# The written order of the attention block and of the layers' first eight steps is drawn anew

## The chip, the cores and the metric

The kernel runs on one core of one Trainium2 chip. The metric is the device time of one execution in microseconds (us), the median of several runs. The engines of the core are TensorE (PE; its weight loads are listed apart as PEld), VectorE (DVE), ScalarE (ACT), GpSimd (POOL) and SyncE (SP), which issues all the DMAs of this kernel. An engine works through its own instructions in their written order; between engines only semaphores order the work.

## What is computed

x has 8 sequences of 1024 rows of 256 numbers. A causal attention block with one head of 64 comes first, then a layer norm; then two layers of local attention (8 heads of 64, windows of 128 rows, each window looks at itself and the one before) with a gated feed-forward part; then a last layer norm. Cut from the reference:

```python
# the attention block
q = x @ wq + bq; k = x @ wk + bk; v = x @ wv + bv
w = softmax(q @ k.T / sqrt(64) + causal_mask)
x = layernorm(x + (w @ v) @ wo + bo)
# two layers, l = 0 and 1
qkv = shift_token(x) @ wqkv[l]
q = rotary(l2norm(q) * q_scale[l]); k = rotary(l2norm(k) * k_scale[l])
x = x + local_attention(q, k, v) @ wo[l]          # window 128 and the one before
h = layernorm(shift_token(x)) * ln_g[l] + ln_b[l]
a, g = split(h @ w1[l] + b1[l])
x = x + (a * gelu(g)) @ w2[l] + b2[l]
# the end
x = layernorm(x1 + x)                              # x1: the input of the layers
```

## The kernel before

All of x is cut into tiles of 128 rows. The attention block works by sequence b (0 to 7) and window j or half n; the layers work by tile T(g), g = 0 to 127: 64 tiles for each of the two layers, and Q(g) is the pair of tiles g and g + 1, which the wide feed-forward products take together.

Each engine has a set of small functions (calls), one for one step of work on one tile. `attention` (from line 188) defines those of the attention block, `layers` (from line 607) those of the layers. On TensorE, the attention has turn_x (transposes of x, L481), project_qk (L491), project_v (L501), scores (L514 and L515), turn_probs (L522), values (L533) and output (L543). scores(b, 4n) waits for the copies of k: ScalarE writes k's high half (k_high), VectorE its low half (k_low), and SyncE copies both to the other 64 partitions (k_high_again at L255, k_low_again at L260). output is followed on VectorE by y_sum (L451), and the next output waits for it, since there is one bank for it. Two banks, turn[0] and turn[1], are shared by turn_x, project_qk, project_v and turn_probs, and each use of one waits until the last one has been read (the waits on `done` in the list).

In the layers TensorE has turn_x (L2486), project_k, project_q, project_v, turn_q, turn_k, scores, turn_probs (L2540), values (L2551), output, turn_h (L2568), widen (in six parts) and narrow. Products of the layers are made of three matmuls each, of high and low halves (`three_pass`, L173 to L175). VectorE takes the rope (rope_cos, rope_sin), norms, the low halves (x_low, q_low, k_low, o_low, h_low, gated_low), least_of for the scores, middle, the statistics and x_new; ScalarE the high halves, the squares, exponentials and gelu; GpSimd inverse_norms, k_sum, k_scaled, normalise and residual.

While the attention runs, the weights of both layers are brought in: SyncE loads them raw (load_raw, L265), ScalarE makes the high half (raw_high), GpSimd the low half (raw_low, L345), SyncE stores both (store_split, L270 and L271), and loads the first layer's part back (load_qkv; first_weights after the attention's last store). The tables of the rope are made on GpSimd (rope_table, L352) and those of the second layer stored (store_tables, L321). Some tiles of the layers lie where tiles of the attention lay. Waits (guards) in the calls of tile 0 keep the order: k_high waits for the stored tables, v_out, probs_out and least_of for all stored splits, o_high, middle and zero_tail for all rows of x1 stored. The second layer's own weight tiles (`next_q_h` and the five like it, loaded by load_next at L756 and following) lie where tiles of the attention lay too.

The order of the work is written out by hand, as a list of calls, for the attention block and the beginning of the layers: `first_on_sync` (L3432), `first_on_gpsimd` (L3691), `first_on_scalar` (L3958), `first_on_vector` (L4535) and `first_on_tensor` (L5468). The last has 727 calls with 647 waits between them. Then `all_steps` runs the function `step` of each engine, from step 8 on SyncE and GpSimd, 9 on ScalarE and VectorE and 11 on TensorE, up to 59, two tiles a step, and `last_steps` is written out again.

## Time and profile before

| | us |
|---|---|
| median of 3 runs | 2685.9 |
| lowest and highest | 2682.23 and 2689.82 |
| the profiled execution | 2684.28 |
| its span, first to last instruction | 2682.5 |
| mean granted TensorE clock | 0.993 |
| TensorE busy, share of the span | 98% |
| VectorE, ScalarE, GpSimd busy | 85%, 72%, 62% |

Busy times are those of the profiled execution. Matmuls are pipelined and their ends are modelled, so that the record of one matmul is longer than the time from its start to the start of the next. Times in the rows below count from the start of the span.

### The profile page before, as it was taken

To read this page: it belongs to the slowest core of one execution; us is meant where nothing else is said; L and a number is where in the kernel's file an instruction comes from. 1 tells how busy PE (TensorE), PEld (TensorE's weight loads), DVE (VectorE), ACT (ScalarE), POOL (GpSimd) and SP (SyncE) were. 2 spreads that over 40 slices of the span, in tenths; PEclk is the share of its full clock that TensorE was granted. 3 is DMA by queue.
4 is the path that set the end of the run, shared out by engine and by line. 5 is a ranking of instruction groups with operands and counts; after the bars stand their busy time and mean duration, and the time that the engine had idled before them with its cause. 6 is when DMAs were issued, how large, how long until landed. Compare 5 with 4: busy or idle time off the path is not lost.

```text
span 2682.5 us, 65519 instructions
## 1 busy us (share of the span) xinstructions
PE 2626.4 (98%) x22240; PEld 2309.2 (86%) x22240; DVE 2276.5 (85%) x6866; ACT 1934.8 (72%) x4826; POOL 1658.1 (62%) x1753
## 2 busy tenths in 40 slices
PE   8999999999999999999999999999999999999998
PEld 5677688899998899998999898989988999988887
DVE  5778988888888888888888889898989989998786
ACT  5655588777777777777777777777777777778775
POOL 6523755566566556666665676666766667766563
PEclk9999999999999999999999999999999999999999
DMA  9931300000001100000001211011101111111110
GB/s 314 334 105 59 107 21 24 29 24 29 27 27 55 44 25 29 25 29 24 28 25 60 93 31 36 30 37 33 37 30 34 33 33 37 31 36 34 30 32 23
DMA packets 144510, 140.37 MB, mean 52 GB/s; under 512 B 16024, under 2 KB 126128, under 8 KB 143408
## 3 DMA queue, kind: packets, MB, share of 16 engines
q1 hardware_dynamic: 144176, 136.18, 16.0%
q8 instruction: 177, 2.90, 0.4%
q14 instruction: 157, 1.29, 0.2%
HBM read 80.02 MB, written 51.92 MB: 49 GB/s over the span
## 4 chain that ended last, share of the span: by engine, by line
PE 61%; DVE 2%; ACT 1%; issue 1%; DMA 1%; SPq 0%; POOL 0%; DVEq 0%; ACTq 0%; POOLq 0%
PE p_pair L173 13%; PE p_pair L174 10%; PE p_pair L175 10%; PE p_values L2551 6%; PE p_turn L2540 5%; PE p_mixed L173 4%; PE p_mixed L175 4%; PE p_mixed L174 4%; PE p_turn L2522 2%; PE p_turn L2516 1%; PE p_mixed L2486 1%; PE p_mixed L2568 1%; PE p_mixed L2594 0%; PE p_mixed L2593 0%; ACT prob L1224 0%
## 5 line engine op out<-in xcount | busy, mean ns | idle before, releaser
L960 POOL TENSOR_TENSOR prob<-prob,rinv 128x512 f32<-128x512 f32 (+1 forms) x512 | 506.5, 1001 | 393.0 <-DVE rinv L1771 392.7
L1224 ACT ACTIVATE prob<-prob,least 128x256 f32<-128x256 f32 (+1 forms) x1024 | 496.2, 487 | 63.2 <-DVE least L1763 61.7
L938 POOL TENSOR_TENSOR inv_norm<-norm_clipped,minus_half 128x8 f32<-128x8 f32 x256 | 423.0, 1659 | 79.2 <-DVE norm_clipped L1727 71.8
L1763 DVE CUSTOM_DVE_ANT_0 prob<-p_pair,mask,inv_norm 128x256 f32<-128x256 f32 (+1 forms) x1024 | 440.2, 460 | 35.0 <-PE p_pair L175 33.0
L173 PE MATMUL p_pair<-hT_h,w_h 128*128 128x256 f32 (+1 forms) x1408 | 410.1, 291 | 6.9 <-ACT v L1218 2.5
L174 PE MATMUL p_pair<-hT_l,w_h 128*128 128x256 f32 (+1 forms) x1408 | 391.1, 278 | 0.0
L175 PE MATMUL p_pair<-hT_h,w_l 128*128 128x256 f32 (+1 forms) x1408 | 391.0, 278 | 0.0
L1236 ACT ACTIVATE pT<-p_turn 128x512 f32<-128x512 f32 (+1 forms) x512 | 283.7, 569 | 76.3 <-PE p_turn L2540 63.9
L173 PEld LDWEIGHTS p_pair<-hT_h,w_h 128*128 128x128 f32 (+1 forms) x1408 | 262.6, 186 | 22.7 <-issue 10.8
L1835 DVE SCALAR_TENSOR_TENSOR gated<-p_pair,columns,gelu 128x256 f32<-128x256 f32 (+1 forms) x384 | 184.0, 481 | 108.5 <-ACT gelu L1263 106.4
L2540 PE MATMUL p_turn<-ident,prob 128*128 128x128 f32 x1920 | 266.5, 273 | 0.8 <-POOL prob L960 0.5
L174 PEld LDWEIGHTS p_pair<-hT_l,w_h 128*128 128x128 f32 (+1 forms) x1408 | 262.9, 187 | 0.0
L175 PEld LDWEIGHTS p_pair<-hT_h,w_l 128*128 128x128 f32 (+1 forms) x1408 | 262.2, 186 | 0.0
L2551 PE MATMUL p_values<-pT,v 128*64 128x128 f32 x3840 | 248.7, 277 | 1.0 <-ACT pT L1236 0.9
L2540 PEld LDWEIGHTS p_turn<-ident,prob 128*128 128x128 f32 x1920 | 220.6, 140 | 26.2 <-issue 10.4
L2551 PEld LDWEIGHTS p_values<-pT,v 128*64 128x64 f32 x3840 | 206.1, 137 | 28.4 <-issue 9.6
L1843 DVE TENSOR_TENSOR gT_l<-gated,gT_h 128x256 fp32r<-128x256 f32 (+1 forms) x384 | 187.6, 490 | 40.1 <-ACT gT_h L1280 38.9
L1263 ACT ACTIVATE gelu<-p_pair,columns 128x256 f32<-128x256 f32 x320 | 150.7, 473 | 92.1 <-PE p_pair L175 91.3
L1711 DVE TENSOR_TENSOR rope_sin<-p_pair,rope_tab 128x256 f32<-128x256 f32 x512 | 199.2, 412 | 0.0
L1224 ACT ACTIVATION_READ_ACCUMULATOR prob<-prob,least 128x1 f32 x1024 | 195.0, 190 | 0.0
L1720 DVE TENSOR_REDUCE norms_sq<-squares 128x8 f32<-128x512 f32 x256 | 173.9, 679 | 24.1 <-ACT squares L1193 23.6
L173 PE MATMUL p_mixed<-w_h,gT_h 128*128 128x256 f32 x640 | 183.4, 287 | 6.1 <-DVE gT_l L1843 3.4
(147 smaller groups left out, 7970.3 us busy)
## 6 DMA issues: line engine op xcount, KB each, us to landing
x_tile<-x_rows SPq DMA_DIRECT2D x192, 128.0 KB, 2.1
a_wraw<-in_w_all SPq DMA_DIRECT2D x32, 264.0 KB, 5.3
w_high<-a_wraw_h SPq DMA_DIRECT2D x32, 264.0 KB, 3.9
w_low<-a_wraw_l SPq DMA_DIRECT2D x32, 264.0 KB, 4.7
a_x<-in_x SPq DMA_DIRECT2D x32, 256.0 KB, 4.2
x_rows<-a_x SPq DMA_DIRECT2D x64, 128.0 KB, 1.8
x_tile<-x_rows SPq DMA_DIRECT2D x128, 64.0 KB, 2.0
mid_rows<-x_mid SPq DMA_DIRECT2D x128, 64.0 KB, 1.7
```

The costliest lines, as they stand in the source:

```text
L173: pe.matmul(out, lh, rh, start=start, stop=False)
L174: pe.matmul(out, lh, rl, start=False, stop=False)
L175: return pe.matmul(out, ll, rh, start=False, stop=stop)
L938: pool.tensor_tensor(r[:, t.slot(2), heads], rt[:, heads], half[:, heads], ALU.pow).then_inc(pool_r[n], 1)
L960: pool.tensor_tensor(p, p, rinv[:, 2 * m:2 * m + 2].unsqueeze(2).to_broadcast([P, 2, cols.stop - cols.start]), ALU.mult).then_inc(pool_p, 1)
L1224: act.activation(prob[:, h, cols], prob[:, h, cols], ACT.Exp, bias=least[:, h:h + 1], scale=-1.0, accum_out=rsum[:, h:h + 1]).then_inc(act ...
L1236: act.activation(pT[:, 2 * m:2 * m + 2, blocks, :], src[:, :, blocks, :], ACT.Copy).then_inc(act_pT, 1)
L1711: ins = dve.tensor_tensor(dst[:, :, s], src[:, :, 1 - s], table[:, 2 * n + 1, s].unsqueeze(1).to_broadcast([P, H, D // 2]), ALU.mult)
L1763: dve.tensor_tensor_reduce(prob[:, h, cols], p_score[h % 2][:, c0 + cols.start:c0 + cols.stop], mask[:, a.slot(2), cols], r[:, a.slot(2), ...
L1843: dve.tensor_tensor(gT_l[0:rows, n], gt[0:rows, n % 3], gT_h[0:rows, n].bitcast(F32), ALU.subtract).then_inc(dve_gT, 1)
L2540: ins = pe.transpose(p_turn[m % 2][:, (2 * hh + b) * P:(2 * hh + b + 1) * P], prob[:, 2 * m + hh, b * P:(b + 1) * P], ident[:])
L2551: ins = pe.matmul(p_val[half_ * D:(half_ + 1) * D, m * P:(m + 1) * P], v[:, slot, h * D:(h + 1) * D], pT[:, h, b], start=b == blocks[0], s ...
```

## The change

Only the five written lists are changed, and the first step of the loop on SyncE. No call is added or taken away: each list has the same calls as before in another order (SyncE's has eight more, which are those of its step 8, and its loop begins at 9). The waits in the list of TensorE go with the calls: each call waits for what its banks and inputs need in the new order. From turn_x(T(13)) on TensorE's list is as it was.

```diff
@@ in post_norm_block @@
-            all_steps(t.step, 8, 60)
+            all_steps(t.step, 9, 60)
@@ first_on_sync @@
     a.load_ident()
+    a.load_bvo()
     a.load_x(0, 0)
-    a.load_wqk()
     a.load_x(0, 1)
     a.load_x(0, 2)
     a.load_x(0, 3)
     a.load_wo()
-    a.load_cmask()
-    a.load_bvo()
+    a.load_wqk()
+    a.load_x(1, 0)
     a.load_wv()
-    a.load_tables()
     a.load_raw(0, 0)
     a.load_raw(0, 1)
+    a.load_tables()
+    a.load_x(1, 1)
     a.load_raw(0, 2)
     a.load_raw(0, 3)
+    a.store_split(0, 0)
+    a.load_x(1, 2)
+    a.load_cmask()
     a.k_high_again(0, 0)
-    a.load_x(1, 0)
-    a.k_high_again(0, 1)
-    a.k_low_again(0, 0)
-    a.load_x(1, 1)
-    a.load_x(1, 2)
-    a.load_x(1, 3)
-    a.k_low_again(0, 1)
-    a.load_x(2, 0)
-    a.store_split(0, 0)
     a.load_raw(1, 0)
-    a.load_shared()
-    a.load_x(2, 1)
     a.load_raw(1, 1)
     a.store_split(0, 1)
+    a.k_low_again(0, 0)
+    a.k_low_again(0, 1)
+    a.load_x(1, 3)
+    a.load_x(2, 0)
+    a.load_x(2, 1)
+    a.k_high_again(0, 1)
     a.load_raw(1, 2)
+    a.load_shared()
     a.load_raw(1, 3)
+    a.load_raw(2, 0)
+    a.load_raw(2, 1)
     a.store_split(0, 2)
-    a.load_raw(2, 0)
     a.store_split(0, 3)
     a.store_split(1, 0)
+    a.store_split(1, 1)
+    a.k_low_again(1, 0)
+    a.store_tables()
     a.k_high_again(1, 0)
```

On TensorE, the head of the new list, where project_v now comes ahead of project_qk:

```python
a.turn_x(0, 0, turn[0])          # as before up to turn_x(0, 3)
...
a.project_v(0, 0, turn[0])
pe.wait_ge(done.xT_done, 4)
a.project_v(0, 1, turn[1])
pe.wait_ge(done.v_done, 1)
a.project_qk(0, 0, turn[0])
pe.wait_ge(done.v_done, 2)
a.project_qk(0, 1, turn[1])
pe.wait_ge(done.kl_done, 1)
a.turn_x(1, 0, turn[0])
pe.wait_ge(done.kl_done, 2)
a.turn_x(1, 1, turn[1])
```

From project_qk(1, 1) to scores(1, 4) in the new list (waits left out; in the old one project_v(1, 1), output(1, 0), project_v(2, 0), project_qk(2, 0), output(1, 1) and turn_probs(1, 2) stood between them):

```python
a.project_qk(1, 1, turn[0])
a.values(0, 6)
a.turn_probs(0, 7, 0, turn[1])
a.output(0, 4)
a.turn_probs(0, 7, 1, turn[1])
a.turn_probs(1, 0, 0, turn[0])
a.output(0, 5)
a.values(0, 7)
a.turn_probs(1, 1, 0, turn[1])
a.turn_probs(1, 2, 0, turn[0])
a.output(0, 6)
a.values(1, 0)
a.scores(1, 4)
```

At the attention's end, the projections of tile 0 and turn_q(T(0)) now stand ahead of scores(7, 5), where they stood behind turn_probs(7, 5), and scores(T(0), 0) stands ahead of output(7, 6), where it stood behind output(7, 7). On GpSimd all rope tables are made ahead of raw_low(1, 2); the last one stood behind raw_low(2, 0). On SyncE the loads of x for tiles 0 to 3 stand behind load_x(3, 1), where they stood behind store_x1(2, 3) and later.

## Rows read from the trace of the kernel before

**Rows 1.** Busy by stretch of 67 us: PE, PEld, DVE, ACT, POOL, PEclk, DMA, GB/s.

```profile
0.00:67.00 67.00, 54.69 (x318) 39.63 (x319) 36.25 (x104) 38.22 (x76) 44.69 (x57) 0.95 0.95 313
67.00:134.00 67.00, 63.20 (x419) 46.30 (x418) 51.22 (x156) 45.57 (x97) 37.05 (x39) 0.95 0.97 334
134.00:201.00 67.00, 62.87 (x448) 47.08 (x446) 49.74 (x159) 36.25 (x78) 20.00 (x27) 0.95 0.34 105
...
268.00:335.00 67.00, 60.56 (x453) 46.50 (x452) 60.74 (x188) 39.22 (x116) 49.62 (x50) 0.95 0.30 107
...
536.00:604.00 68.00, 68.00 (x582) 61.24 (x582) 58.51 (x179) 49.95 (x131) 40.90 (x42) 1.00 0.09 25
```

**Rows 2.** TensorE's waits up to 700 us: line <- releaser, us, times, longest.

```profile
PE p_turn L481 <- DMA a_x<-in_x: 8.1, 3, 3.9
PE p_mixed L543 <- DVE a_y L451: 5.1, 7, 1.7
...
PE p_pair L514 <- DMA a_k_low_twice<-a_k_low_twice: 2.4, 3, 1.8
```

**Rows 3.** Timeline from 9 us: start, duration, engine, line, operation [idle before it].

```profile
14.61 0.59 SPq L247 DMA_DIRECT2D a_x<-in_x  x1
...
15.78 0.59 SPq L260 DMA_DIRECT2D a_k_low_twice<-a_k_low_twice  x1
...
22.03 0.90 PE L481 MATMUL p_turn<-ident,a_x 128*128 128x128 f32 x4 [2.72 <-DMA a_x<-in_x]
...
23.31 0.44 PE L514 MATMUL p_pair<-a_k_high_twice,a_q_high_low 128*128 128x128 f32 x1 [0.38 <-DMA a_k_low_twice<-a_k_low_twice]
```

**Rows 4.** Busy by microsecond behind that wait; the third number from the end is PEclk.

```profile
23.00:24.00 1.00, 0.69 (x3) 0.72 (x4) 0.00 (x0) 0.56 (x1) 1.00 (x2) 0.50 1.08 355
...
30.00:31.00 1.00, 1.00 (x12) 1.00 (x11) 0.39 (x4) 0.71 (x1) 1.00 (x1) 1.00 1.06 406
```

**Rows 5.** Timeline of TensorE: project_qk(1, 0), and two matmuls of a layer's projection.

```profile
33.48 1.88 PE L491 MATMUL p_turn<-a_xT,a_wqk 128*128 128x512 f32 x4
...
1003.09 0.40 PE L173 MATMUL p_pair<-wqkv_h,xT_h 128*128 128x512 f32 x1
1003.33 0.39 PE L174 MATMUL p_pair<-wqkv_l,xT_h 128*128 128x512 f32 x1
```

**Rows 6.** Timeline of TensorE: turn_x of tiles 0, 13, 14 and 16.

```profile
244.61 0.42 PE L2486 MATMUL p_mixed<-ident,x_tile 128*128 128x128 f32 x2
...
481.83 0.38 PE L2486 MATMUL p_mixed<-ident,x_tile 128*128 128x128 f32 x2
506.57 0.38 PE L2486 MATMUL p_mixed<-ident,x_tile 128*128 128x128 f32 x2
...
543.73 0.38 PE L2486 MATMUL p_mixed<-ident,x_tile 128*128 128x128 f32 x2
```

**Rows 7.** VectorE up to 300 us, by line: busy us, mean ns, idle before.

```profile
L451 DVE SCALAR_TENSOR_TENSOR a_y<-p_mixed,a_rinv,a_x_plus_bo 128x256 f32<-128x256 f32 x64 | 30.7, 480 | 11.5 <-PE p_mixed L543 5.7 <-issue 5.4
```

**Rows 8.** Busy by stretch at the attention's end, columns as in group 1.

```profile
270.00:280.00 10.00, 6.45 (x47) 4.60 (x46) 9.78 (x27) 1.68 (x3) 5.84 (x6) 0.91 0.11 39
280.00:290.00 10.00, 9.46 (x68) 6.97 (x66) 9.89 (x38) 6.66 (x24) 6.28 (x9) 0.92 0.29 92
```

**Rows 9.** Timeline from 80 us: project_qk(2, 1), table store, k copy, scores(2, 4).

```profile
81.16 1.98 PE L491 MATMUL p_turn<-a_xT,a_wqk 128*128 128x512 f32 x4
81.59 0.61 SPq L321 DMA_DIRECT2D rope_tables<-a_tab_layer  x1
...
86.98 0.48 SPq L260 DMA_DIRECT2D a_k_low_twice<-a_k_low_twice  x1
...
92.56 0.47 PE L514 MATMUL p_pair<-a_k_high_twice,a_q_high_low 128*128 128x512 f32 x1 [1.76 <-DMA a_k_low_twice<-a_k_low_twice]
```

**Rows 10.** The copies of k's low half in the whole run, from issue to landing.

```profile
DMA to landing us min/median/max: 2.2/3.3/7.4
```

**Rows 11.** DMA issues of the first 150 us: KB each, median us to landing.

```profile
a_k_low_twice<-a_k_low_twice SPq DMA_DIRECT2D x10, 128.0 KB, 4.5
```

More of the change, by code:

```diff
@@ L5491, in first_on_tensor @@
     a.turn_x(1, 2, turn[0])
+    pe.wait_ge(done.xT_done, 6)
+    a.project_v(1, 0, turn[1])
+    a.scores(0, 0)
+    a.scores(0, 1)
+    pe.wait_ge(done.xT_done, 7)
+    a.project_qk(1, 0, turn[0])
+    pe.wait_ge(done.v_done, 3)
+    a.turn_x(1, 3, turn[1])
     a.scores(0, 2)
@@ L5554, in first_on_tensor @@
+    a.scores(1, 5)
+    a.values(1, 1)
     a.output(0, 7)
[L5555 to L5569 removed]
@@ L5588, in first_on_tensor @@
-    pe.wait_ge(done.pT_done, 17)
+    a.turn_x(2, 1, turn[1])
+    a.scores(1, 7)
+    a.values(1, 2)
+    pe.wait_ge(done.xT_done, 9)
+    a.turn_probs(1, 4, 0, turn[0])
+    a.output(1, 0)
+    pe.wait_ge(done.xT_done, 10)
+    a.project_qk(2, 0, turn[1])
+    a.values(1, 3)
+    pe.wait_ge(done.pT_done, 17)
+    a.project_v(2, 0, turn[0])
+    a.output(1, 1)
+    pe.wait_ge(done.kl_done, 5)
+    a.turn_probs(1, 4, 1, turn[1])
+    a.output(1, 2)
+    pe.wait_ge(done.v_done, 5)
     a.turn_probs(1, 5, 0, turn[0])
-    a.output(1, 3)
@@ L5744, in first_on_tensor @@
+    a.project_v(4, 1, turn[1])
+    a.output(3, 6)
+    a.values(4, 0)
+    pe.wait_ge(done.pT_done, 50)
     a.turn_x(5, 0, turn[0])
-    pe.wait_ge(done.pT_done, 48)
+    a.scores(4, 6)
+    pe.wait_ge(done.v_done, 10)
     a.turn_x(5, 1, turn[1])
-    a.values(3, 7)
-    a.output(3, 6)
+    a.output(3, 7)
+    a.values(4, 1)
+    a.scores(4, 7)
     pe.wait_ge(done.xT_done, 21)
-    a.turn_x(5, 2, turn[0])
+    a.turn_probs(4, 2, 0, turn[0])
     pe.wait_ge(done.xT_done, 22)
-    a.project_qk(5, 0, turn[1])
@@ new lines, in first_on_tensor @@
+    pe.wait_ge(done.pT_done, 58)
+    a.project_qk(5, 0, turn[1])
+    pe.wait_ge(done.pT_done, 59)
+    a.project_qk(5, 1, turn[0])
+    a.output(4, 5)
+    a.values(4, 6)
+    pe.wait_ge(done.kl_done, 11)
+    a.turn_probs(4, 7, 1, turn[1])
+    a.output(4, 6)
+    pe.wait_ge(done.kl_done, 12)
+    a.turn_x(6, 0, turn[0])
+    a.values(4, 7)
+    pe.wait_ge(done.pT_done, 60)
+    a.turn_x(6, 1, turn[1])
+    a.scores(5, 0)
+    pe.wait_ge(done.xT_done, 25)
+    a.turn_x(6, 2, turn[0])
+    a.scores(5, 1)
@@ L5953, in first_on_tensor @@
-    pe.wait_ge(done.v_done, 16)
-    a.turn_probs(7, 3, 0, turn[1])
-    a.values(7, 2)
+    t.project_k(T(0), 0)
+    a.values(7, 0)
+    pe.wait_ge(done.v_done, 15)
+    a.turn_probs(7, 1, 0, turn[0])
+    pe.wait_ge(done.v_done, 16)
+    a.turn_probs(7, 2, 0, turn[1])
+    a.scores(7, 4)
+    t.project_k(T(0), 1)
+    a.output(7, 0)
+    a.values(7, 1)
+    pe.wait_ge(done.pT_done, 86)
+    a.turn_probs(7, 3, 0, turn[0])
+    pe.wait_ge(done.s_low, 60)
+    t.after((signal.dve_xT, T(0), 1, 1))
@@ L6048, in first_on_tensor @@
     t.turn_probs(T(0), 3)
+    t.after((signal.dve_xT, T(2), 1, 1))
+    t.turn_x(T(3))
+    pe.wait_ge(done.zT_done, 64)
+    t.after((signal.act_pT, T(0), 4, 1))
+    t.values(T(0), 0)
+    t.after((signal.act_pT, T(0), 4, 2))
+    t.values(T(0), 1)
     t.after((signal.dve_kr, T(2), 1, 1))
@@ L6261, in first_on_tensor @@
+    t.scores(T(6), 1)
+    t.after((signal.dve_hv, Q(2), 1, 1))
+    t.narrow(T(0))
     t.after((signal.act_pT, T(5), 4, 1))
```

3010 lines of the change are left out of this document (1474 added, 1536 removed).

## The prediction

> **What bounds the kernel now.** I read four views, in this order. First the busy times of stretches of 67 us [rows 1]: TensorE is busy all the time from 536 us on, and the places where it is not (12.3 us idle in the first stretch, 3.8 in the second, 4.1 in the third, 6.4 in the fifth) all lie in the part whose order is rewritten. Second, who ended TensorE's idle time there [rows 2]: loads of x, the attention's y, the copy of k's low half. Third, the clock: after the 2.72 us of idle time that end at 22.03 us [rows 3] the granted clock reads 0.50, the lower of its two levels (1.2 GHz for 2.4), and 1.00 again by 30 us [rows 4]. Four of the first five stretches of 67 us have a mean of 0.95 [rows 1]: 0.05 x 67 x 4 = 13.4 us of work not done.
>
> Fourth, a count, because busy time is too coarse for a change that moves calls and removes none. I give each TensorE call the time between its first matmul and the next call's in dense rows: 0.235 us for a 512-column three-pass matmul, so 1.45 for a whole projection; 1.75 for project_qk and 1.9 for the attention's project_v, read like them [rows 5]; found in the same way: scores of window j 0.10 + 0.117(j + 1), values 0.10 + 0.06(j + 1), a transpose 0.115, output 0.5 in the attention and 1.46 in the layers, widen 1.42, narrow 2.05. The 727 written calls make 507.5 us in either order. Over two tiles of the steady part the count gives 37.4 us, and the trace 37.16 (506.57 to 543.73 [rows 6]), so it can be trusted to 1%. Time of the trace minus work counted is the **slip** of TensorE. It is 54.0 us at tile 0's turn_x (244.61 - 190.6), 83.3 at tile 13's (481.83 - 398.5) and 83.1 at tile 16's (543.73 - 460.6) [rows 6]: all of it arises before tile 13, and from tile 13's turn_x on both orders are the same, call by call. Of the 83, some 34 are idle time and 13 the clock; about 36 are waits too short for a row of their own, switches between kinds of matmul, and errors of my call times in the attention. So the change can win at most some 45 to 50 us and will surely leave most of them.
>
> The Trainium skill says in "Perfetto Trace Analysis", section "Identifying the Most-Contended Engine", that occupancy of the matmul row is no measure of headroom, while that of VectorE is. The trace agrees: in the fifth stretch TensorE is 90% busy [rows 1], and the slip still grows by some 12 us. By busy time alone the sum below would have a ceiling of some 34 us, by the slip one of 83.
>
> **VectorE in the written order.** I count VectorE the same way, with the mean times of its groups (0.48 for a y_sum [rows 7], 0.46 + 0.08 for a least of the layers, and so on), and take for each wait of TensorE the VectorE work written up to the result that it waits for, minus the TensorE work written before the call. This **lead** may rise and fall without harm as long as VectorE has idle time; where it rises and VectorE is full, TensorE slips by the rise. In the old order it is 1.6 us or less for the first 140 us of work, 9.3 at the turn_x of tile 1, 24.3 at project_v of tile 2 and 33.5 at its highest, project_v of tile 9. VectorE is indeed 98% and 99% busy from 270 to 290 us [rows 8], and the slip rises there from 57 to 69 us.
>
> **The change, part by part** (sum against the profiled execution: 2684.28 us with a span of 2682.5; the median of the three runs, 2685.9, is 1.6 above it).
>
> *The first 30 us.* project_v now goes ahead of project_qk. The biases that it needs (160 KB) are issued ahead of x(0,0), which delays that by one issue, about 0.45 us; wqk moves behind four loads of x and two of wo and still lands before it is needed; x(1,0) is issued before all raw weights and not behind them (before: issued at 14.61, waited for until 22.03 [rows 3]). Going through the calls by hand, with 0.68 us for each half of q or k on ScalarE and 0.75 on VectorE (their groups' means), turn_x(1,0) starts at about 18.6 with 9.2 us of work behind it (slip 9.4; before 12.8), and scores(0,0) at 24.0 if the k copies have landed. They are issued at about 19.4 behind raw loads and splits; the first low copy took 7.5 us before (15.78 to 23.3 [rows 3]), so they land between 24 and 27. The slip there is 11.5 to 14.5; the old order has 15.9 at 13.9 us of work. Gain 1.4 to 4.4 us; I take **-3.0**, the middle.
>
> *The copies of k.* scores(b, 4n) needs both halves of k copied, and the work written between project_qk(b, n) and it is the cover. The chain can be timed at (2,1): from the end of the product (81.16 + 1.98) to the copy's arrival (92.5) 9.4 us, 5.6 of them the low half's own flight, and scores(2,4) waited 1.76 us [rows 9] with a stretch of low clock behind it (3.3 us of work). This came right behind the 1 MB store of the rope tables (81.59 [rows 9]), which now goes out some 50 us earlier. The flight is 2.2 us at least and 7.4 at most, its median 3.3 over the run [rows 10] and 4.5 in the first 150 us [rows 11], where the DMA engines are full [rows 1]. (2,1) keeps its cover (6.7 us, now 6.8): with 4.5 its chain is 8.3 and the wait shrinks to some 0.6, mostly without the clock; -5.0 if all goes, 0 if all stays, I take -4. (1,1) had 6.95 us of cover and now 4.6, stretched by the usual slip to 5.4: with 4.5 a wait of 2.9, and the clock's 3.3 may follow; between 0 (flight 2.2) and 4.0 + 3.3 (chain as at (2,1)). I take 2.9 and half the clock's, +4.5. (3,0) falls from 9.4 to 5.8, (5,0) from 11.2 to 5.3 and (6,1) from 9.1 to 4.5, but from 134 us on the DMA engines are a third busy or less, and the old (4,0) had 5.2 without a row of idle time: +1.5 together, between 0 and 6. The part: **+2.0**, between -5 and +13.
>
> The Trainium skill's "DMA: Bandwidth & Descriptors", section "Queues, rings and completion order", has the descriptors of one queue on one engine start in order. The trace agrees (15.78 to 23.3 us for a copy behind a load [rows 3]). It speaks against this part, as SyncE now issues k_high_again(0,1) behind three loads of x.
>
> *The rest of the attention.* Outputs that follow each other too closely for the y between them (under 0.9 us of work) fall from nine to seven; turn_x to the projections gets shorter in places. No row prices this: **0**, between -3 and +3, from the 5.1 us that outputs waited for y in all [rows 2].
>
> *From the attention's end to tile 13.* The lead rises from 10.2 (output(7,2)) to 32.5 (turn_q of tile 6), by 22.3 us, before from 9.3 to 33.5, by 24.2. At project_v of tile 3 it is 25.9, in the old order 23.7. VectorE's work is the same and it is full here, so most of this slip stays: **-2.0**, between -6 (the small waits of 0.8 to 1.1 us after 350 us go too) and +3 (tile 2's project_k has 0.7 us of work behind its turn_x, before 2.0, and ScalarE and VectorE need 0.8 in between by their groups' means).
>
> *Hidden edits.* The rope tables on GpSimd (16 x 0.73 us) move ahead of raw_low of the second batch; SyncE waits for the last of them in store_tables, with k_high_again(1,0) queued behind it, but scores(1,0) now has 10.5 us of cover for 6.3. The loads of x for tiles 0 to 3 and the last wqkv loads move within the time before 150 us, and their first reader is at 240 us. The first layer weights, loaded from 290 us on, still wait for the attention's last store, with nothing reordered around it. The eight calls of step 8 on SyncE are written out and not looped. All at 0; if a cover failed, a load's flight of 2 to 4 us.
>
> Sum: -3.0 + 2.0 + 0 - 2.0 = -3.0, so 2681.3 us by the profiled execution and 2682.9 beside the median. **I predict 2682 us**, between the two, its own range 2676 to 2690.
>
> **The rivals.** (A) *The low clock goes as well.* If neither the load of x nor the k copies stop TensorE for over 1.5 us at a stretch, three stretches of low clock vanish (3.35 us of work each) with 2.72 + 1.76 us of idle time before two of them and 1.2 before the third: 15.7 in all, of which the attention's end gives back some 3 because VectorE is full: 2684.3 - 12.7 = 2671.6, and beside the median 2673 us. For it: the gaps before 22 and 92.6 us have one cause each, and both are moved. Against: shorter cover for k. (B) *The k copies become the bound, slower than before.* If they fly 5 us or more behind the raw loads, (1,1) and (3,0) each wait 2.5 to 3 us and drop the clock (3.3), 12 us for the two, scores(2,4) waits as before, and the copy for scores(0,0) lands at 27 us, which leaves 1.4 of the head's gain: +12 - 1.4 - 2 (the layers) = +8.6, 2694.5 us beside the median. It decides from a flight of 4.5 us on; the median of the whole run is below that [rows 10], that of the first 150 us upon it [rows 11]. (C) *VectorE keeps all.* What the attention gains is given back by 300 us, since VectorE has 39 us of work there for 26 of TensorE's: 2686 us, no change.
>
> **How the numbers follow.** My forecast 0.37, C 0.20, A 0.27, B 0.16. A measurement of this kernel can tell about 0.3% (8.1 us) from no change: faster means below 2677.8, slower above 2694.0. Nearly all of A is faster, with a little of the forecast's edge, 0.29; most of B is slower with little else, 0.14; the rest is 0.57. For 8 times in 10 the range takes in A's middle and B's near half: 2670 to 2695.
>
> **What the profile would show.** Right: no idle time of over 1 us on a load of x near 22 us; a wait of TensorE on the k copy at scores(1,4) of 2 to 4 us, and at most a small one at scores(2,4); VectorE over 95% busy around 270 to 290 us; tile 13's turn_x at a slip of 79 to 82 us, which is 478 to 480 us in the trace; from there on the same 37.16 us for two tiles. Wrong: a new wait on a k copy in each batch, or a store or load on SyncE that stands in front of them; a low clock that stays away altogether; a change of the steady part, on which everything here is set to zero.

## The result, and the profile after

The changed kernel takes 2697.3 us in the median of six executions (2689.5 to 2701.1), the old one 2685.4 beside it (2682.2 to 2689.8). The ratio is 1.0038 with a 95% interval of 1.0026 to 1.0049: **slower** by 7 to 13 us. The forecast was 2682, between 2670 and 2695, with 0.14 for slower.

The profiled execution of the changed kernel took 2689.5 us and is the fastest of its six, so a good part of the loss is not in it. Its page:

```profile
span 2687.7 us, 65516 instructions
...
PE 2618.9 (97%) x22240; PEld 2307.1 (86%) x22240; DVE 2276.1 (85%) x6866; ACT 1929.1 (72%) x4820; POOL 1658.1 (62%) x1753
```

The transposes (turn_x) of tiles 0, 13, 14 and 16 in the timeline of TensorE answer to [rows 6] (start, duration, engine, line):

```profile
240.54 0.38 PE L2486 MATMUL p_mixed<-ident,x_tile 128*128 128x128 f32 x2
...
485.17 0.38 PE L2486 MATMUL p_mixed<-ident,x_tile 128*128 128x128 f32 x2
...
509.89 0.38 PE L2486 MATMUL p_mixed<-ident,x_tile 128*128 128x128 f32 x2
...
547.03 0.38 PE L2486 MATMUL p_mixed<-ident,x_tile 128*128 128x128 f32 x2
```

By the count of the prediction tile 0 stands behind 188.2 us of work in the new order, tiles 13, 14 and 16 behind 398.5, 423.2 and 460.6 as before. The slip is 240.54 - 188.2 = 52.4 us at tile 0 (old 54.0), 86.6 at tile 13 (old 83.3) and 86.4 at tile 16. So here the attention is 1.6 us better, **the layers' first 13 tiles are 5.0 us worse** (34.3 us of slip against 29.3), and the steady part still takes 37.14 us for two tiles. All along the loop from there to tile 126 the two traces keep 2.6 to 3.8 us apart. The last 2 us come at the very end, where the last products of the new trace run at a lower granted clock (0.81 from 2670 to 2680 us, old 1.00) on the same instructions.

TensorE's waits between 300 and 485 us, old kernel first, then the changed one (line <- releaser: us in all, times, longest):

```profile
PE p_pair L173 <- ACT v L1218: 1.9, 2, 1.1
PE p_pair L173 <- DVE rope_sin L1711: 1.4, 2, 0.8
PE p_pair L173 <- DVE gated L1835: 1.1, 1, 1.1
PE p_mixed L173 <- DVE x_new L1855: 0.5, 1, 0.5
```

```profile
PE p_pair L173 <- DVE gated L1835: 3.2, 3, 1.7
PE p_pair L173 <- ACT v L1218: 2.2, 1, 2.2
PE p_pair L173 <- DVE rope_sin L1711: 2.0, 4, 0.8
PE p_pair L173 <- DVE kT_l L1746: 1.2, 1, 1.2
PE p_pair L173 <- DVE least L1763: 1.0, 2, 0.7
PE p_pair L173 <- DVE xT_l L1691: 1.0, 1, 1.0
PE p_turn L2540 <- POOL prob L960: 0.9, 1, 0.9
```

With the small ones that are left out, 5.7 us of waits became 14.0. The slip rose by 5.0 only, so some of them stand in the place of waits too short for a row. None is long; they are spread over all three engines that read TensorE's banks. But they do not weigh the same. At the transposes of tile 11 the slip is some 80 us in the new trace (430.59 us, behind 351 of work) and some 82 in the old one (437.95, behind 356): the new order is still ahead. From there to tile 13 it grows by some 7 us, in the old trace by 1. In the 20 us behind tile 11's transposes ScalarE is full, and VectorE and TensorE are not (new trace, columns as in [rows 1]):

```profile
430.00:440.00 10.00, 8.26 (x76) 6.98 (x72) 8.93 (x30) 9.88 (x19) 6.86 (x8) 1.00 0.01 2
440.00:450.00 10.00, 7.28 (x54) 5.87 (x54) 5.44 (x17) 9.90 (x21) 2.62 (x3) 1.00 0.01 2
```

In the same 20 us of the old trace TensorE is full, and VectorE nearly so:

```profile
430.00:440.00 10.00, 10.00 (x86) 8.97 (x86) 9.79 (x24) 6.00 (x15) 8.49 (x7) 1.00 0.16 48
440.00:450.00 10.00, 10.00 (x82) 8.44 (x79) 9.68 (x30) 9.19 (x22) 3.34 (x5) 1.00 0.13 35
```

The old order has such a stretch too, from 410 to 430 us (ScalarE 97% and 96% busy, TensorE 89% and 91%). The two largest waits of the new trace stand 4 us apart:

```profile
434.96 0.47 ACT L1263 ACTIVATE gelu<-p_pair,columns 128x256 f32<-128x256 f32 x1
...
435.94 1.28 ACT L1224 ACT_TABLE_LOAD   x1
...
438.16 1.28 ACT L1263 ACT_TABLE_LOAD   x1
...
439.46 0.47 ACT L1263 ACTIVATE gelu<-p_pair,columns 128x256 f32<-128x256 f32 x1
...
439.96 0.48 DVE L1835 SCALAR_TENSOR_TENSOR gated<-p_pair,columns,gelu 128x256 f32<-128x256 f32 x1
...
440.50 0.50 PE L173 MATMUL p_pair<-wqkv_h,xT_h 128*128 128x512 f32 x1 [1.73 <-DVE gated L1835]
...
443.57 0.71 ACT L1280 ACTIVATE gT_h<-gated 128x256 fp32r<-128x256 f32 x2
...
444.18 0.58 ACT L1218 ACTIVATE v<-p_pair 128x512 f32<-128x512 f32 x1
...
444.81 0.37 PE L173 MATMUL p_pair<-hT_h,w_h 128*106 128x256 f32 x1 [2.21 <-ACT v L1218]
```

Read from the bottom: the sixth widen product of tiles 4 and 5 needs the bank of tile 10's v, which ScalarE copies out at 444.18, behind two exponentials, a k_high and two gated_high, though the last matmul of the product was done by 442.2 (441.77 + 0.39). And v's own product could start only at 440.50, since its bank held a widen product whose gated was late, whose gelu had waited for two table loads on **ScalarE**. In the old list project_v(T(10)) stood in front of the third widen product, here it stands between the fifth and the sixth.

### The profile page after: what moved, and what is told of

Its sections match the earlier page's. It is cut to its first block, busy times and chain, and to the rows that moved or that the text cites. A ratio compares the mean times of both kernels' runs of the same rounds, so it can differ in the third digit from the quotient of the medians.

```text
span 2687.7 us, 65516 instructions
## 1 busy us (share of the span) xinstructions
PE 2618.9 (97%) x22240; PEld 2307.1 (86%) x22240; DVE 2276.1 (85%) x6866; ACT 1929.1 (72%) x4820; POOL 1658.1 (62%) x1753
## 4 chain that ended last, share of the span: by engine, by line
PE 61%; DVE 2%; ACT 2%; issue 1%; DMA 1%; SPq 0%; POOL 0%; DVEq 0%; ACTq 0%; POOLq 0%
PE p_pair L173 13%; PE p_pair L174 10%; PE p_pair L175 10%; PE p_values L2551 6%; PE p_turn L2540 5%; PE p_mixed L173 4%; PE p_mixed L175 4%; PE p_mixed L174 4%; PE p_turn L2522 2%; PE p_turn L2516 1%; PE p_mixed L2486 1%; PE p_mixed L2568 1%; PE p_mixed L2594 0%; PE p_mixed L2593 0%; ACT prob L1224 0%
## 5 line engine op out<-in xcount | busy, mean ns | idle before, releaser
L1224 ACT ACTIVATE prob<-prob,least 128x256 f32<-128x256 f32 (+1 forms) x1024 | 495.9, 487 | 60.1 <-DVE least L1763 58.6
L173 PEld LDWEIGHTS p_pair<-hT_h,w_h 128*128 128x128 f32 (+1 forms) x1408 | 262.7, 187 | 21.7 <-issue 10.3
```

The source lines that it names most:

```text
L173: pe.matmul(out, lh, rh, start=start, stop=False)
L1224: act.activation(prob[:, h, cols], prob[:, h, cols], ACT.Exp, bias=least[:, h:h + 1], scale=-1.0, accum_out=rsum[:, h:h + 1]).then_inc(act ...
```

## The experiments

For each trace I worked out the slip as in the prediction, from the turn_x of tiles 0, 6 and 13 and the order in the kernel's list. This table holds the study's traces (A: attention, L: layers from the output product of tile 0 on; "new" with an edit is marked):

| trace | A, L | slip at tile 0 | 0 to 6 | 6 to 13 |
|---|---|---|---|---|
| before | old, old | 54.0 | 17.4 | 11.9 |
| before_look | old, old | 52.0 | 19.5 | 12.2 |
| short_before | old, old | 53.9 | 17.4 | 11.8 |
| after | new, new | 52.4 | 18.0 | 16.3 |
| after_again | new, new | 55.2 | 18.0 | 16.3 |
| after_look2 | new, new | 61.3 | 18.0 | 16.3 |
| after_look3 | new, new | 55.6 | 18.0 | 16.3 |
| short_after | new, new | 58.2 | 18.0 | 16.3 |
| att_after_lay_before | new, old | 58.9 | 17.4 | 12.2 |
| old_layers_look | new, old | 58.4 | 17.1 | 12.2 |
| old_layers_look2 | new, old | 59.0 | 15.8 | 12.2 |
| att_before_lay_after | old, new | 54.2 | 23.8 | 16.3 |
| restore_from_tile5 | new, new to tile 5 | 54.0 | 25.6 | 13.8 |
| v10_early | new, new edited | 60.0 | 19.9 | 18.4 |
| gelu_grouped | new, new edited | 55.9 | 19.1 | 21.0 |
| head_alone | old with new head, old | 57.2 | 17.3 | 11.9 |
| old_head | new with old head, new | 60.2 | 18.0 | 16.3 |
| bvo_later | new edited, new | 57.2 | 18.0 | 16.3 |
| warm_start | new edited, new | 58.6 | 18.0 | 16.3 |
| old_layers_warm | new edited, old | 59.2 | 15.8 | 12.2 |

### Where the loss is: the lists cut and joined

At some points the calls written so far are the same set in both orders, on each engine. There a list of the one order can go on as the other.

```diff
 # att_after_lay_before (att_before_lay_after: the other way round)
 def first_on_tensor: new order up to t.output(T(0)), t.turn_k(T(2)), t.turn_probs(T(1), 0)
-    (new) t.values(T(1), 0), t.turn_probs(T(1), 1), t.turn_probs(T(1), 2), ...
+    (old) t.values(T(1), 0), t.turn_probs(T(1), 1), t.scores(T(2), 0), ...
 # restore_from_tile5: the same behind t.project_v(T(5))
```

after_again, the changed kernel as it is:

> The changed kernel once more, nothing edited. Its median stood at 2697.3 us (six executions, 2689.5 to 2701.1) and its one profiled execution at 2689.5, so some 8 us of the loss are in no trace yet. Theory L (layers): the loss is fixed work order in tiles 5 to 12 of the layers; then the spread is chance, the median comes again at 2695 to 2699, and a second trace shows tile 13's transposes at 484 to 487 us. Theory K (copies of k): the loss is in the attention and changes with how long the copies of k take to land; then a slower profiled execution has the transposes of tile 0 later than 240.5 us by about what it is slower.

Measured: 2697.7 us, ratio 1.0037 (1.0025 to 1.0049); the profiled execution 2692.8. The loss repeats. The trace is 2.8 us later than the first at tile 0, and from there equal to it within 0.1 us: both theories had a part right, the layers cost a fixed amount and the attention a varying one.

> The changed kernel up to the output product of the layers' tile 0 (about 300 us), from there the old order on all five engines. Theory L: the waits of 1.7 and 2.2 us for gated and v near 440 us go, tile 13's transposes come 3 to 5 us earlier than in the changed kernel (480 to 482 us), and the time is 2692 to 2694 us. Theory K: what is lost is lost before 300 us, and the time stays at 2696 to 2698.

Measured: 2686.7 us, ratio 1.0002 (0.9993 to 1.0010). **The whole loss is gone with the old order of the layers**, and more of it than theory L asked for.

```profile
247.05 0.38 PE L2486 MATMUL p_mixed<-ident,x_tile 128*128 128x128 f32 x2
...
486.93 0.38 PE L2486 MATMUL p_mixed<-ident,x_tile 128*128 128x128 f32 x2
```

Tiles 0 and 13 in its trace: 239.88 us apart, in the changed kernel 244.63. In the table this is 29.6 us of slip against 34.3. But this trace took 2692.3 us, the slowest of its eleven.

> The mirror image: the old order up to the output product of the layers' tile 0, from there the new one. Theory L: 2689 to 2692 us, with the waits near 440 us in the trace. Theory K: 2685 to 2688 us, since the old attention has its copies of k in time.

Measured: 2696.6 us, ratio 1.0038 (1.0026 to 1.0050). The new layers bring the loss along with the old attention: for L, against K. The time is 5 us above what L said, and the trace shows why this kernel is no clean measure: it loses 23.8 us between tiles 0 and 6, where the pure orders lose 17.4 (19.5 in before_look) and 18.0. Some 1.5 us of the excess arise ahead of the join, where the clock is low for longer (from 278 to 288 us, as in before_look), the rest behind it. From tile 6 on it has the 16.3 of the new order.

> The changed kernel with the old order restored only from about the value product of the layers' tile 5 on (370 us), so that only the stretch with the waits near 440 us is as before. Theory L: as the kernel restored from tile 0 on, 2692 to 2694 us, and tile 13's transposes at 480 to 482 us. Theory K: 2696 to 2698 us.

Measured: 2698.1 us, ratio 1.0046 (1.0034 to 1.0058). By itself this would say K. The trace says otherwise: 25.6 us between tiles 0 and 6 (18.0 without a join), with the excess at the join (a wait of 2.7 us for x_mid with a stretch of low clock behind it), and then 13.8 in place of 16.3. The experiment is spoilt by its join and settles nothing on size.

### Why executions of one kernel differ

> The changed kernel once more, for a trace of one of its slower executions. Its two traces so far (2689.5 and 2692.8 us) took 19.3 to 21.1 us less of TensorE work away between the transposes of tiles 2 and 6 than time went by less than the mixed kernel did, and lie below the median of 2697.5. Theory W (waits of the layers' tiles 2 to 6): a slower execution loses 4 to 7 us more between the transposes of tiles 2 and 6 (time beyond counted work 8.3 in both traces, then 13 to 15, as in the kernel with the old attention and the new layers), by waits and a lower clock together. Theory K: it loses them before tile 0's transposes (52.4 and 55.2 us beyond counted work, then 58 to 60).

> The same kernel and the same two theories as the run before it: W puts what is above 2692 us between the transposes of tiles 2 and 6, K ahead of tile 0's.

(The first text has a muddled sentence; what counts in it is 8.3 us between tiles 2 and 6 for W and 58 to 60 at tile 0 for K.) Measured: 2698.3 and 2692.6 us. All five traces of the new order have 18.0 and 16.3 us, to 0.1; the slow one has 61.3 us at tile 0. **W is wrong, K right** as to where the variation arises, ahead of tile 0. But it isn't the copies of k: up to 245 us TensorE waits 3.6 us for them in the slow trace and 3.9 in the changed kernel's first one, while its waits for pT ahead of turn_probs go from 1.9 to 4.7 us. Part of the variation arises in the first 25 us. TensorE's timeline there, the changed kernel's first trace and then after_look2 (v is L501, q and k L491):

```profile
6.25 3.74 PE L481 MATMUL p_turn<-ident,a_x 128*128 128x128 f32 x16 [6.25 <-DMA a_x<-in_x]
...
9.99 3.92 PE L501 MATMUL p_turn<-a_wv,a_xT 128*128 128x64 f32 x32
13.75 3.65 PE L491 MATMUL p_turn<-a_xT,a_wqk 128*128 128x512 f32 x8
18.81 0.66 PE L481 MATMUL p_turn<-ident,a_x 128*128 128x128 f32 x4 [1.41 <-DVE a_k_low_twice L416]
```

```profile
10.60 7.06 PE L501 MATMUL p_turn<-a_wv,a_xT 128*128 128x64 f32 x32 [0.34 <-DMA a_wv<-in_wv]
17.45 6.24 PE L491 MATMUL p_turn<-a_xT,a_wqk 128*128 128x512 f32 x8
24.31 0.66 PE L481 MATMUL p_turn<-ident,a_x 128*128 128x128 f32 x4 [0.62 <-DVE a_k_low_twice L416]
```

The same 32 matmuls take 3.92 or 7.06 us, 0.12 or 0.22 each. Of the 15 traces that begin with the new head, seven have 3.8 to 4.1 us, seven 7.06, and one (warm_start) 4.59. The slow heads reach their next transposes at 22.8 to 24.3 us, 4.0 to 5.5 later. The old head has no such levels: its five traces have 4.3 to 5.2 us for q and k and 2.00 for the first 16 matmuls of v. What the pace is, the traces tell (last section): it is the granted clock, whose record opens with full speed at 9.5 to 11.0 us in the seven heads with v in 3.8 to 4.1 us, at 18.7 to 22.6 in the seven with 7.06 and at 11.3 to 12.4 in the five old ones.

Two more edits and the mirror image of the head were to show whether this makes the times.

```diff
 # head_alone: old kernel, new order of the first calls (TensorE 8, SyncE 31, GpSimd 15, ScalarE 12, VectorE 7)
 # old_head: the changed kernel with the old order of the same calls
 # bvo_later, first_on_sync
-    a.load_bvo()
     a.load_x(0, 0)
     a.load_x(0, 1)
     a.load_x(0, 2)
     a.load_x(0, 3)
+    a.load_bvo()
 # warm_start, turn_x(0, 0), behind the wait for the identity (old_layers_warm: new attention
 # and old layers, with 6 of them and bvo_later's edit)
+                for m in range(14):
+                    pe.transpose(turn[1][:, m % 4 * P:(m % 4 + 1) * P], ident[:], ident[:])
```

> The old kernel with the new order of the head alone: on all engines up to the first sequence's q, k and v products (first 8 calls on TensorE, 31 on SyncE, 15 on GpSimd, 12 on ScalarE, 7 on VectorE); the first two transposes after it wait for the low half of k as well. My forecast's step: the head gives 1.4 to 4.4 us, so 2681.5 to 2684.5. The rival: bvo ahead of x(0,0) holds the first transposes 2.3 us later and k comes after v, so it gives nothing or costs up to 3 us, 2686 to 2689.

Measured: 2687.7 us beside 2686.0, ratio 1.0007 (0.9998 to 1.0016); 57.2 us of slip at tile 0, v in 7.06 us. The head gives nothing; whether it costs is within the interval (-0.5 to +4.3 us). The rival's side.

> The changed kernel with one call of SyncE moved: bvo is loaded behind the four pieces of x of the first sequence, no longer ahead of them. In the traces of the changed kernel the first transposes start at 6.1 to 6.7 us (old kernel: 3.95), and the 32 matmuls of the first v products take either 3.8 to 4.1 us or 7.06 us. Theory P (pace of the head): whether TensorE works at full pace at 10 us or only at 20 us makes the two levels of the changed kernel's times (2689 to 2693 and 2697 to 2701); with work from 4 us on it is at full pace by 12 us, the slow level goes, and the median falls to 2688 to 2692. Rival: only the 2.3 us of later start count, and the median falls to 2694 to 2696 with both levels left.

Measured: 2692.3 beside 2683.2 on this chip, ratio 1.0034 (1.0022 to 1.0045). The first transposes start at 4.07 us, as said, but v takes 7.06 us all the same. An earlier start doesn't bring the full pace. The ratio is hardly under that of the changed kernel.

> The changed kernel with 14 transposes of the identity added on TensorE ahead of the first transposes of x, while it waits for x anyway (from 2.6 us, when the identity is there, to about 6 us). They compute nothing that is used. Theory P: TensorE has been at work from 2.6 us on, the first v products take 3.8 to 4.1 us in the trace, the slow level goes, and the median is 2689 to 2693. Rival: the two levels have another cause, and the median stays at 2696 to 2699.

Measured: 2694.8, ratio 1.0040 (1.0023 to 1.0057), executions from 2687.0 to 2702.3. TensorE was at work from 2.80 us, v took 4.59 us, and then q and k 6.22, at the low pace. The added work did bring full pace early, from 6.8 us on, but it was lost again: the granted clock is low from 13.6 to 20.4 us. Theory P in this form is wrong: work ahead of time doesn't keep the pace.

> The changed kernel with the old order of the head (to the first sequence's q, k and v products on all engines); the first two transposes after it wait for v as well. Theory P: with its first transposes at 4 us, the old head comes to full pace by 12 us each time, and the median falls from 2697.5 to 2689 to 2693, leaving the 4.9 us of the layers' part. By the rival, that the new head is no worse than the old one, it stays at 2696 to 2698.

Measured: 2696.2, ratio 1.0049 (1.0036 to 1.0063), the highest of all. With the old head's pace (v in 2.00 + 2.00 us) the trace still has 60.2 us of slip at tile 0. It is late already at scores(1,0), 48.39 us for 44.30 in the old kernel, with the same calls up to 22 us; this is one trace, and the join behind the head may have a part in it. So the head's two levels explain the spread of the traces in part, not the loss.

> The kernel with the new attention and the old layers (median 2686.7), with bvo loaded behind x and 6 transposes of the identity ahead of the first of x. By theory P the head begins 2.3 us earlier and at full pace: 2682 to 2685, below both kernels. If the head's time is taken up by later waits, it stays at 2686 to 2688.

Measured: 2689.4, ratio 1.0022 (1.0014 to 1.0031). Not below either kernel, and above the same layers without the head's edits (1.0002).

### The waits near 440 us

```diff
 # v10_early, first_on_tensor (v_out(T(10)) on ScalarE moves to behind squares(T(10), 0))
     t.project_q(T(10))
     t.after((signal.dve_gt, Q(4), HF + 1, 2))
-    t.project_k(T(10), 0)
+    t.project_v(T(10))
...
     t.scores(T(9), 0)
+    t.after((signal.act_v, T(10), 1, 1))
+    t.project_k(T(10), 0)
     t.project_k(T(10), 1)
...
-    t.project_v(T(10))
...
     t.widen(Q(4), 5)
 # gelu_grouped: that, and in first_on_scalar
+    t.exponential(T(9), 3)
     t.gelu(Q(4), 2)
-    t.exponential(T(9), 3)
...
     t.gelu(Q(4), 4)
+    t.gelu(Q(4), 5)
```

The first half of project_k(T(10)) shares the bank with v, so it moves behind the copy of v, to after scores(T(9), 0).

> The changed kernel with one call put back: TensorE makes the value product of the layers' tile 10 right after that tile's q product, as in the old order, and not between the fifth and the sixth widening product of the pair of tiles 4 and 5; ScalarE copies it out accordingly. If the place of this call makes the waits of 1.7 us (gated) and 2.2 us (v) near 440 us, then both go, tile 13's transposes come 2.5 to 4 us earlier in the trace, and the median falls from 2697.5 to 2693.5 to 2695. If VectorE and ScalarE are behind there anyway, TensorE waits somewhere else for as long and the median stays at 2696.5 to 2698.

Measured: 2695.9, ratio 1.0033 (1.0020 to 1.0046); tiles 6 to 13 have 18.4 us, more than 16.3. TensorE's waits from 430 to 492 us:

```profile
PE p_values L2551 <- ACT pT L1236: 2.8, 1, 2.8
PE p_pair L173 <- DVE gated L1835: 2.1, 1, 2.1
```

The wait for v is gone, one for pT has come, and a stretch of low clock behind it. The other side of the expectation: the engines are behind there, not one call. ScalarE more than VectorE: it is 91% busy from 440 to 450 us and 91% from 450 to 460, VectorE 84% and 46%.

> The kernel with tile 10's value product put back (its trace waits 2.1 us for gated and 2.8 us for pT near 455 us), and on ScalarE two more calls moved: the fourth exponential of tile 9 ahead of the third gelu of the pair 4 and 5, and the sixth gelu right behind the fifth, so that gelus and exponentials stand in groups. Each switch between the two costs a table load of 1283 ns; the changed kernel has 8 of them between 425 and 460 us, the kernel with the old layers 5. Theory T (table loads): ScalarE is late there by its table loads; with 4 fewer, both waits go, the time beyond counted work between the transposes of tiles 6 and 13 falls from 16.3 us to 12 to 14, and the median stands 3 to 5 us under the changed kernel's, at 1.0020 to 1.0028 of the old kernel. Rival: VectorE is what is late; 16 to 18 us beyond counted work remain there, and the ratio stays at 1.0033 to 1.0040.

Measured: 2697.3 beside 2687.5, ratio 1.0034 (1.0021 to 1.0048); 21.0 us from tile 6 to 13, some 3.4 of them the low clock (0.66 from 450 to 460 us). The same waits:

```profile
PE p_values L2551 <- ACT pT L1236: 4.3, 1, 4.3
PE p_pair L173 <- DVE gated L1835: 2.3, 2, 1.5
```

and ScalarE, with its gelus side by side:

```profile
444.90 0.47 ACT L1263 ACTIVATE gelu<-p_pair,columns 128x256 f32<-128x256 f32 x1 [0.45 <-PE p_pair L175]
447.81 0.47 ACT L1266 ACTIVATE gelu<-p_pair,columns 42x256 f32<-42x256 f32 x1 [2.44 <-PE p_pair L175]
448.30 1.28 ACT L1224 ACT_TABLE_LOAD   x1
449.60 0.51 ACT L1224 ACTIVATE prob<-prob,least 128x256 f32<-128x256 f32 x1
```

Theory T, that fewer loads take the waits away, falls. Its count was off as well: the changed kernel has 7 loads from 425 to 460 us, not 8, and from 330 to 485 us it has 16 where the old one has 22. There are fewer table loads here, but the sixth gelu, put forward, makes ScalarE stand for 2.44 us, and the exponentials and pT behind it are late by more than was saved. ScalarE isn't full any more (67% and 57% from 440 to 460 us), and TensorE waits longer: the number of loads alone is not the cause, the order of ScalarE's calls counts too. (The Trainium skill, "ScalarE: Activation LUTs", section "What ACT_TABLE_LOAD costs", has 1283 ns for one. The trace agrees. It has a drain of 1380 ns with each switch as well; in the rows above the exponential starts at 449.60 us, right behind the load, and the measurement decides.) The chain near 440 us runs TensorE, ScalarE, VectorE, TensorE through one bank, and these two repairs only moved the wait along it.

### How much of it the traces show

> The kernel with the new attention and the old layers once more, for a trace. Its median (2686.7) is 11 us below that of the changed kernel, but the one trace of it accounts for 4.7 us (between the transposes of tiles 0 and 13: 29.6 us beyond counted work against 34.3). If the rest is chance of the attention (52.4 to 61.3 us beyond counted work at tile 0 in the traces of the same order), this trace has again 29.6 us there and 52 to 59 at tile 0. If the old layers save more than that trace shows, it has under 27 us between tiles 0 and 13.

> The same kernel and the same two readings as the run before it: 29.6 us between the transposes of tiles 0 and 13 and a varying start, or under 27 us there.

> The old kernel once more, for a second trace of its own attention. Its first has 54.0 us beyond counted work at tile 0's transposes and 29.3 from there to tile 13's; two traces with the same attention order had 54.2 and, with the new head, 57.2. If the old attention varies less than the new, it comes at 53 to 55 and 29.3.

Measured: 2692.4, 2689.7 and 2687.9 us. The mixed kernel has 29.3 and 28.0 us from tile 0 to 13 and 58.4 and 59.0 at tile 0. So the old layers do not save more than the first trace showed, and the first reading holds as far as traces go. before_look has 52.0 at tile 0, and 31.8 us to tile 13 in place of 29.3, the rest of it in a stretch of low clock from 270 to 300 us.

But a gap remains. The three traced executions of this kernel took 2689.7 to 2692.4 us; the other ten of its first eleven lie between 2682.0 and 2688.4. For the changed kernel it is the other way: traced 2689.5, 2692.6, 2692.8 and 2698.3, nine others 2693.0 to 2701.1 with a median of 2697.7. So the traces are no fair sample of the timed executions. The last two kernels make the written lists most of the time.

```diff
 # short_before, short_after
-            all_steps(t.step, 9, 60)
-            t.last_steps()
+            all_steps(t.step, 9, 17)
...
-        return Tile(g) if 0 <= g < TILES else None
+        return Tile(g) if 0 <= g < 24 else None
```

(on each engine; TensorE also waits for the last reader of a bank in the last four tiles. These two kernels compute only a part, without the output.)

> The old kernel cut short: the layers' loop stops after tile 23 of 128 (24 tiles of the first layer; the last steps and the second layer with the final norm are left out, and with them the output), so that the written lists make up most of the time, some 700 us. For comparison with the next one, of which only the order differs.

> The changed kernel cut short in the same way. Reading 1: all that the change costs, 11 us by the medians of the whole kernels, is lost ahead of tile 16; then the medians of the two short kernels differ by 9 to 12 us. Reading 2: what the traces show up to tile 13 is all there is in the lists (5 us in the layers, 0 to 3 in the attention), and the rest comes from the loop or from chance; then they differ by 4 to 8 us.

Measured: 753.0 us (751.3 to 755.5) and 764.8 us (758.9 to 765.6), **11.8 us apart**: reading 1. So the loss of the whole kernels is there without the loop behind step 16. Tiles 0 and 13, short_before and then short_after:

```profile
244.44 0.42 PE L2489 MATMUL p_mixed<-ident,x_tile 128*128 128x128 f32 x2
...
481.59 0.38 PE L2489 MATMUL p_mixed<-ident,x_tile 128*128 128x128 f32 x2
```

```profile
246.34 0.38 PE L2489 MATMUL p_mixed<-ident,x_tile 128*128 128x128 f32 x2
...
491.03 0.38 PE L2489 MATMUL p_mixed<-ident,x_tile 128*128 128x128 f32 x2
```

This pair of traces (753.7 and 765.1 us) is as far apart as the medians: 4.3 us of slip at tile 0 (58.2 - 53.9; a slow head with 7.06 us for v), 5.1 from there to tile 13, and the rest, 2.0, behind it, where the short kernels drain. Such a drain the whole kernels do not have at this place, so 9.4 of the 11.4 us are those of the lists.

## Why the prediction was wrong

**What bounds the kernel.** TensorE's slip ahead of tile 13 was the right quantity: the steady part stayed at 37.14 us, and the two short kernels have the whole difference within 24 tiles. The sum of the terms, -3.0, came out as +8.7 in the traces: the head and the attention, priced at -1.0, gave +3.7, and the layers up to tile 13, priced at -2.0, gave +5.0. The second is the larger miss, and there the working was against the wrong partner (below).

**The first 30 us, -3.0.** Wrong in sign. The hand walk was right for the fast head up to one call: turn_x(1,0) was put at 18.6 us and came at 18.81, in the seven fast traces at 18.8 to 19.4. That is in part luck: the first transposes came 1.9 us later than priced and this call only 0.2, so that something in between was priced too high by about as much. Three terms failed. bvo ahead of x(0,0) was priced at one issue, 0.45 us; the transfer itself stood in front, and the first transposes came at 6.25 us and not at 3.95, 2.3 us later. The matmuls were priced at one pace, where seven of 15 traces have v at 7.06 us. And the walk had no wait behind turn_x(1,0): the next transposes waited 2.77 us for the low half of k (at 22.24 us), a stretch of low clock followed (0.50 from 21 to 30 us), and scores(0,0), put at 24.0, came at 27.54. At scores(1,0), behind 25 us of work in both orders, the new attention stands at 43.2 to 44.8 us in the fast traces and 45.4 to 48.8 in the others, the old one at 44.3 to 44.6: nothing gained, up to 4 us lost, **+1.2** on the mean of the eleven traces named below. head_alone: +1.7 us, -0.5 to +4.3.

**The copies of k, +2.0.** The waits came out near the sum, not where it put them: scores(1,4) waited 0.50 us (at 60.47) for 2.9, and three others up to 130 us waited 1.28, 1.03 and 1.16. In all 4.0 us against 2.4 before [rows 2]. The low clock behind the wait at scores(2,4) [rows 9] is gone in three of the four traces of the whole changed kernel. The copies' flight was at the edge, as feared: its median is 4.7 us in the first 150 us, 4.5 before, and 8.1 at most.

**The rest of the attention, 0.** It isn't 0, though small in sum. From scores(1,0) to scores(4,0) the new order loses 4.0 us more than the old one, 1.5 to 7 in single traces; in the changed kernel's first trace the copies of k have 1.6 us of more waits in all, and TensorE waits for the z of output and for pT as well (1.7 us ahead of output and 1.0 ahead of turn_probs from 44 to 142 us, none and 0.4 before). From scores(4,0) to tile 0 it wins 1.5 of it back. With the copies' +2.0 this makes +2.5. The attention as a whole, priced at -1.0, has 57.2 us on the mean of eleven traces with the new order (the changed kernel's four, short_after, the three of the mixed kernel, restore_from_tile5, v10_early and gelu_grouped; 52.4 to 61.3) against 53.5 on that of four with the old one: **+3.7**. By the times of the kernel with the old layers it is +0.5, between -1.9 and +2.7. These two don't agree.

**From the attention's end to tile 13, -2.0, between -6 and +3.** This is the step that made most of the error: **+5.0**, outside of its own bounds (34.3 us in all five traces of the new order, 29.2 and 29.3 in two of the old one; before_look has 31.8, with more low clock). It went by the lead of VectorE alone, and this did ease as forecast: from 270 to 290 us VectorE is 77% and 89% busy, where [rows 8] has 98% and 99%.

```profile
270.00:280.00 10.00, 9.16 (x82) 6.95 (x82) 7.71 (x28) 3.74 (x11) 4.79 (x4) 1.00 0.01 2
280.00:290.00 10.00, 8.10 (x59) 6.00 (x58) 8.86 (x33) 5.88 (x19) 5.09 (x9) 1.00 0.16 54
```

(columns as in [rows 1].) The granted clock is 1.00 there too, for 0.91 and 0.92. At tile 6 the trace was 1.0 us better than the old one (70.4 for 71.4), and the forecast would have been near. Nearly all is lost between tiles 6 and 13, 16.3 us for 11.9, and within that behind tile 11, where ScalarE is 99% busy for 20 us, VectorE 89% and 54%, and TensorE 83% and 73% (rows above). ScalarE is 99% busy from 440 to 450 us in the changed kernel's three other traces, in short_after and in att_before_lay_after too; att_after_lay_before, with the old layers, has 73% there and 96% in the next 10 us, with TensorE full in both, so a full ScalarE alone does not make the loss. ScalarE's calls, with the 1283 ns of a table load at each switch between exponential and gelu, were in no sum: a term put at nothing without a reason. What a lead of this kind needs is the same count for ScalarE and GpSimd, and for each bank the chain through all its readers. The bound of +3 was taken from one place (tile 2's project_k), while twelve tiles of new order had none.

**The rivals.** B was nearest in time (2694.5) with another mechanism: its flight came true, but no copy was waited for as long as it said. A's mechanism came true in part and gained nothing: the stretch of low clock from 160 us is gone in all four traces of the whole changed kernel (two have one of 3.4 us from 147 us on) and that from 90 us in three, and up to 500 us the clock costs 6.8 to 10.2 us in these for 13.6 in both old ones (10 us times what the clock lacks, summed, without the start of the program, which the record leaves out), but longer sums of short waits stand in their place. C, that VectorE keeps all, is refuted by the rows above.

**What the profile was to show.** No wait of over 1 us on a load of x near 22 us: right, but 2.77 us on the low half of k at 22.24. A wait of 2 to 4 us at scores(1,4): 0.50, wrong. VectorE over 95% busy around 270 to 290 us: wrong. Tile 13 at 478 to 480 us: 485.2. The steady part unchanged: right.

**What stays open.** That the new order of the layers' tiles loses is shown by traces and times alike, the size isn't the same: about 5 us in the traces, 11 us between the medians of the changed kernel and of the one with old layers. The sum of the traces, 3.7 + 5.0 = 8.7 us, lies inside of the measured 7 to 13. Why traced executions of the mixed kernel are slower than timed ones, and why the clock is granted at 10 us in one execution and at 19 to 23 in the next, I can't say. Nor is it shown why the attention's middle, from scores(1,0) to scores(4,0), loses 1.5 us in one execution and 7 in another. That ScalarE is full where the layers lose is shown; that its order makes the loss is not proven by a repair: the two edits meant to do so only showed that moving single calls does not help.

## What to carry to other kernels

When an order is rewritten, count the lead for every engine that empties TensorE's banks, not for the busiest one: here VectorE, the busiest after TensorE, had slack to give where the loss arose, and ScalarE, in no sum, was full. Where a forecast's terms are 2 to 4 us and executions differ by 10, take several traces and compare time beyond counted work stage by stage: four traces of one kernel agreed to 0.1 us in the stage that had lost, while their totals spread over 9 us. Lists joined from two orders can pay at the join (some 5 and 7 us in two of three here, nothing in the third), so look at the trace of a hybrid before its time is believed.

## What was unexpected of the hardware

TensorE began at half its pace and stayed there through up to 16 us of all but unbroken work (6.51 to 22.6 us in after_look2). The granted clock of those stretches reads 1.00, but nothing is recorded there. The clock entries in the trace begin only with the first rise to full speed, at 10.3 us in the changed kernel's first trace and at 22.6 in after_look2, and the time from one matmul to the next halves at just these points: from 0.21 to 0.11 us around 10.4 us, and from 0.85 to 0.43 at 22.7. So what comes ahead of the first entry is the lower of the two levels, and the spacing of matmuls has to be read there. From 10 to 13 us, the changed kernel's first trace and then after_look2 (columns as in [rows 1]; the first has 26 matmuls in this time, the second 14):

```profile
10.00:13.00 3.00, 3.00 (x26) 3.00 (x26) 0.42 (x1) 1.24 (x2) 1.12 (x1) 1.00 0.99 332
```

```profile
10.00:13.00 3.00, 2.66 (x14) 2.43 (x12) 0.11 (x2) 1.37 (x4) 1.15 (x1) 1.00 1.00 374
```

The Trainium skill, in "TensorE: Matmul & The Clock Gate", Part 1, has the engine start at the lower rate and leave it once it has been busy. The traces with v in 3.8 to 4.1 us agree. Those with 7.06 do not fit that simple picture: they stay at the lower level through 13 to 16 us of work, all but unbroken in five of the seven. In warm_start, with 14 transposes from 2.80 us on, the clock rose at 6.8 us, and after a run of transposes with gaps (0.16, 0.25 and 0.78 us of idle time before 8.61, 9.48 and 10.89 us) it fell at 13.6 us, in the midst of dense work on v. Here the record shows it:

```profile
14.00:20.00 6.00, 6.00 (x13) 3.41 (x14) 0.42 (x1) 0.93 (x2) 2.95 (x4) 0.50 1.02 331
```

So the early work brought no lasting gain.
